# Last stage of a graph layer: every quad as fp32r halves, and the scaled x stored once in fp32

## The reference

```python
def lap_mul(A, x):
    d = 1.0 / sqrt(sum(A, axis=-1))
    return d[:, None] * (A @ (d[:, None] * x))

z = leaky_relu(lap_mul(A, x) @ W1 + b1, 0.1)
d2 = max(sq[:, None] + sq[None, :] - 2 * z @ z.T, 0)   # sq: row sums of z * z
S = exp(-sqrt(d2 + 1e-10) / 2)                       
S = where(rank of S in its row < 4, S, 0)              # the four nearest nodes
out = layernorm(x + lap_mul(S + A, x) @ W2 + b2)
```

## Time and profile before

| | us |
|---|---|
| Median of 3 runs | 2693.22 (2692.01 to 2697.63) |
| Span of the profiled execution | 2759.5 |
| of it, last stage (first rounding to the end) | 2242 to 2760 |
| TensorE busy in the span | 90% |
| VectorE busy in the span | 84% |
| ScalarE busy in the span | 58% |
| GpSimd busy in the span | 43% |

### The profile page before, as it was taken

One profiled execution on the slowest core, in us unless ns is written; L12 is line 12 of the kernel. 1 busy time (PEld: TensorE's weight loads), 2 busy tenths in 40 slices (PEclk: granted clock), 3 DMA queues, 4 the chain that ended last, 5 costly groups with the idle time before them and its releaser, 6 DMA issues.

```text
span 2759.5 us, 29107 instructions
## 1 busy us (share of the span) xinstructions
PE 2482.6 (90%) x9356; PEld 1722.4 (62%) x9356; DVE 2319.8 (84%) x1411; ACT 1606.7 (58%) x1905; POOL 1195.4 (43%) x987
## 2 busy tenths in 40 slices
PE   1367999999999998899999999999999987888978
PEld 0133444444677776578787877778787764666655
DVE  7998899977788888999999999999999773666766
ACT  0000000000477767999989899899988763555655
POOL 0000000000000000377778878788878956666760
PEclk9688999999999999999999999999999988999989
DMA  9999999995899960146555655555655688988975
GB/s 385 421 402 408 398 421 421 421 421 215 320 349 342 338 226 7 35 141 183 151 163 138 179 142 175 140 170 149 174 143 167 182 309 343 347 324 320 345 295 208
DMA packets 147949, 718.58 MB, mean 260 GB/s; under 512 B 19025, under 2 KB 26961, under 8 KB 86609
## 3 DMA queue, kind: packets, MB, share of 16 engines
q1 hardware_dynamic: 124384, 670.49, 65.6%
q0 software_dynamic: 18800, 37.77, 5.7%
q10 hardware_dynamic: 4608, 8.39, 0.8%
HBM read 680.40 MB, written 36.18 MB: 260 GB/s over the span
## 4 chain that ended last, share of the span: by engine, by line
PE 56%; issue 10%; ACT 10%; DVE 9%; DMA 7%; POOL 3%; another core or an unknown queue 3%; SPq 0%; ACTq 0%; POOLq 0%; DVEq 0%
PE PS L767 17%; PE PS L866 5%; PE PS L868 5%; PE PS L867 5%; DMA ring<-at 4%; ACT R L1141 3%; PE PS L834 3%; PE PS L910 3%; PE PS L921 3%; PE PS L911 3%; PE PS L830 2%; PE PS L831 2%; ACT ah_t L1191 2%; DVE R L1621 2%
## 5 line engine op out<-in xcount | busy, mean ns | idle before, releaser
L1299 POOL TENSOR_TENSOR al<-ring,ah 128x1024 fp32r<-128x1024 f32 x264 | 644.0, 2441 | 180.5 <-ACT ah L1112 168.7
L1621 DVE MAX8 R<-R 128x8 f32<-128x8192 f32 x64 | 555.9, 8685 | 68.1 <-ACT R L1141 67.9
L1141 ACT ACTIVATE R<-PS 128x1024 f32<-128x1024 f32 x512 | 518.1, 1018 | 114.1 <-PE PS L874 83.1
L1624 DVE FIND_INDEX8 R<-R,R 128x8 uint32<-128x8192 f32 x64 | 555.9, 8685 | 0.3 <-issue 0.3
L1272 POOL CAST zst<-zh 128x128 fp32r<-128x128 f32 (+1 forms) x64 | 26.2, 410 | 1113.2 <-DVE zl L1556 811.5
L866 PE MATMUL PS<-zh,zst 128*128 128x512 f32 x1024 | 407.3, 398 | 28.6 <-ACT PS L1127 12.7
L868 PE MATMUL PS<-zh,zst 128*128 128x512 f32 x1024 | 400.4, 391 | 0.0
L867 PE MATMUL PS<-zl,zst 128*128 128x512 f32 x1024 | 400.1, 391 | 0.0
L1456 POOL DMA_INDIRECT R<-xs_dram,R x256 | 279.7, 1093 | 145.2 <-issue 75.5
L1127 ACT ACTIVATE PS<-R 128x1024 f32<-128x1024 f32 x310 | 318.0, 1026 | 6.6
L1046 ACT ACTIVATE tiny<-rowsum 128x4 f32<-128x4 f32 x16 | 3.3, 205 | 481.2 <-DVE rowsum L1491 481.2
(11 more groups left out here) (177 smaller groups left out, 4469.9 us busy)
## 6 DMA issues: line engine op xcount, KB each, us to landing
R<-at SPq DMA_DIRECT2D x152, 1024.0 KB, 13.3
ring<-at SPq DMA_DIRECT2D x148, 1024.0 KB, 9.5
ring<-at SPq DMA_DIRECT2D x264, 512.0 KB, 3.9
cache<-at SPq DMA_DIRECT2D x117, 1024.0 KB, 20.2
raw_sq<-at SPq DMA_DIRECT2D x21, 1024.0 KB
raw_z<-at SPq DMA_DIRECT2D x20, 1024.0 KB
raw_ring<-at SPq DMA_DIRECT2D x20, 1024.0 KB
acc_dram<-R POOLq DMA_DIRECT2D x78, 256.0 KB, 5.7
```

The source lines that it names most:

```text
L1141: act.activation(score[j % 2][:, c * EC:(c + 1) * EC].rearrange("p (b c) -> p b c", b=2), pair(first, j, c), ACT.Copy).then_inc(copied, 1)
L1299: pool.tensor_tensor(al[:, k % SPLIT], raw[k % RAW], ah[:, k % SPLIT].bitcast(F32), ALU.subtract)\
L1621: v.max(top[:, j], score[j % 2]).then_inc(dve3, 1)
L1624: v.max_index(place[:, j], top[:, j], score[j % 2]).then_inc(placed, 1)
```

## The change

1. All 124 quads of the last stage are halved. The plain branch is gone, and with it the bookkeeping of places. For the last group, ACT makes the high half of xg (`high_of_last`, after quad 4's rounding) and DVE the low half (`low_of_last`, ahead of quad 5's).
2. In the third stage, SP writes the scaled x of a group twice in fp32 (once in the layout for the gathers, once as it lies on chip, `xp_dram`) in place of once plus both halves, and reads the next x only when both have landed. POOL's wait for the writes of the halves is gone.
3. In the last stage, SP reads one 512 KB piece for a group in place of two. ACT makes its high half (`high_of_xs`), POOL its low half (`low_of_xs`) in place. POOL's six later low halves stand between its other work: two ahead of the write of the last group's x, one ahead of the gathers, and three behind the 4th, 16th and 28th gather.

```diff
+LOW_AFTER = {4: (0, 0), 5: (0, 3), 6: (1, 2)}
...
-                        dst = xh_dram[bass.ds(g, 1)].rearrange("o p t d -> p (o t) d")
-                        sp.dma_start(dst, xgh_g[:, :, :].bitcast(F32)).then_inc(s_split, 16)
-                        dst = xl_dram[bass.ds(g, 1)].rearrange("o p t d -> p (o t) d")
-                        sp.dma_start(dst, xgl_g[:, :, :].bitcast(F32)).then_inc(s_split, 16)
+                        dst = xp_dram[bass.ds(g, 1)].rearrange("o p t d -> p (o t) d")
+                        sp.dma_start(dst, xg).then_inc(s_xp, 16)
                     if k == RAW + (NP0 // 2 if first else 0):
                         sp.wait_ge(s_xg, 16 * (g + 1))
+                        sp.wait_ge(s_xp, 16 * (g + 1))
...
             def load_t(u):
-                if u >= RAW_T and plain[u - RAW_T]:
-                    sp.wait_ge(prod_t, u - RAW_T + 1)
-                elif u >= RAW_T:
+                if u >= RAW_T:
                     wait_rest(sp, u - RAW_T)
...
             def load_xs(g):
-                sp.dma_start(xsh[:, g * GT:(g + 1) * GT].bitcast(F32), xh_dram[g]).then_inc(s_xs[g], 16)
-                dst = (xsl if g < G - 2 else xsh)[:, low * GT:(low + 1) * GT].bitcast(F32)
-                sp.dma_start(dst, xl_dram[g]).then_inc(s_xs[g], 16)
+                sp.dma_start(low_tiles(g).bitcast(F32), xp_dram[g]).then_inc(s_xs[g], 16)
...
             def quad(u):
-                if plain[u]:
-                    pe.wait_ge(xg_ok, chain_of(G - 1, False))
-                    pe.wait_ge(ld_t[u % RAW_T], 16 * (u // RAW_T + 1))
-                    for k in range(TB):
-                        i = pe.matmul(bank, xg[:, (h * TB + k) % GT], raw_t[u % RAW_T][:, k], ...)
-                    i.then_inc(prod_t, 1)
-                    return
-                pe.wait_ge(s_xs[h * TB // GT], 32)
-                pe.wait_ge(rnd_t, n + 1)
+                if h >= LAST:
+                    pe.wait_ge(xl_last_ok, 1)
+                else:
+                    pe.wait_ge(xs_low, h * TB // GT + 1)
+                pe.wait_ge(rnd_t, u + 1)
...
+            def high_of_last():
+                act.wait_ge(xg_ok, chain_of(G - 1, False))
+                act.activation(xgh_of[1][:, :, :], xg, ACT.Copy).then_inc(xh_last_ok, 1)
+            def high_of_xs(g):
+                act.wait_ge(s_xs[g], 16)
+                act.activation(xsh[:, g * GT:(g + 1) * GT], low_tiles(g).bitcast(F32), ACT.Copy).then_inc(xs_high, 1)
+            high_of_xs(0)
             for u in range(len(tail)):
-                if not plain[u]:
-                    round_t(u)
+                round_t(u)
+                for g in range(1, G - 1):
+                    if u == tail.index((HB, g * GT // TB)) - 1:
+                        high_of_xs(g)
...
+                if u == BY_POOL + 2:
+                    high_of_last()
...
-                    pool.wait_ge(s_split, 32 * (g - 1))
-                    hold(pool)
...
+            def low_of_xs(g):
+                pool.wait_ge(xs_high, g + 1)
+                pool.tensor_tensor(low_tiles(g), low_tiles(g).bitcast(F32), xsh[:, g * GT:(g + 1) * GT].bitcast(F32),
+                                   ALU.subtract).then_inc(xs_low, 1)
+            low_of_xs(0)
             for u in range(BY_POOL):
...
+            low_of_xs(1)
+            low_of_xs(2)
             pool.wait_ge(xg_ok, chain_of(G - 1, False))
             pool.dma_start(dst.rearrange("(t p) d -> p t d", p=P), xg).then_inc(s_xg_last, 16)
+            low_of_xs(3)
...
+                    for g, after in LOW_AFTER.items():
+                        if (f, j) == after:
+                            low_of_xs(g)
...
+            def low_of_last():
+                v.wait_ge(xh_last_ok, 1)
+                v.tensor_tensor(xgl_of[1][:, :, :], xg, xgh_of[1][:, :, :].bitcast(F32), ALU.subtract)\
+                 .then_inc(xl_last_ok, 1)
...
+                if u == BY_POOL + 3:
+                    low_of_last()
-                if not plain[u]:
-                    rest_t(u)
+                rest_t(u)
```

More of the change, by code:

```diff
@@ L126, in plan_tail, with build @@
     return quads
-def build(nc, x, at, W1, b1, W2, b2, consts, out, xs_dram, xh_dram, xl_dram, acc_dram):
+def build(nc, x, at, W1, b1, W2, b2, consts, out, xs_dram, xp_dram, acc_dram):
     loads, products, two = plan_ab()
@@ L288, in build, with high_tile, low_tiles @@
             raw_t.append(sb(name, [P, TB, BC], at=where)[:, :, :])
+        def high_tile(t):
+            return xsh[:, t] if t < (G - 1) * GT else xgh_of[1][:, t % GT]
+        def low_tiles(g):
+            low = g if g < G - 2 else G - 1
+            return (xsl if g < G - 2 else xsh)[:, low * GT:(low + 1) * GT]
         def low_tile(t):
+            if t >= (G - 1) * GT:
+                return xgl_of[1][:, t % GT]
             return xsl[:, t] if t < (G - 2) * GT else xsh[:, t + GT]
@@ L376, in build @@
         flushed = sem("flushed")
-        s_split = sem("s_split")
+        s_xp = sem("s_xp")
+        xs_high = sem("xs_high")
+        xs_low = sem("xs_low")
         s_xs = [sem(f"s_xs{k}") for k in range(G - 1)]
@@ L391, in build @@
         acc_seeded = sem("acc_seeded")
+        xh_last_ok = sem("xh_last_ok")
+        xl_last_ok = sem("xl_last_ok")
         rnd_t = sem("rnd_t")
@@ L521, in build @@
         n_heavy = [f + 1 - n_light[f] for f in range(B)]
-        plain = [h >= LAST for b, h in tail]
-        halved = [u for u in range(len(tail)) if not plain[u]]
-        place_of = {u: n for n, u in enumerate(halved)}
         def wait_rest(eng, u, part_=RESTS - 1):
-            if place_of[u] < BY_POOL:
-                eng.wait_ge(al_pool, place_of[u] + 1)
+            if u < BY_POOL:
+                eng.wait_ge(al_pool, u + 1)
             else:
-                eng.wait_ge(al_dve, RESTS * (place_of[u] - BY_POOL) + part_ + 1)
+                eng.wait_ge(al_dve, RESTS * (u - BY_POOL) + part_ + 1)
         def wait_halves_free(eng, u):
-            if place_of[u] >= 2:
-                eng.wait_ge(prod_t, halved[place_of[u] - 2] + 1)
+            if u >= 2:
+                eng.wait_ge(prod_t, u - 1)
         def wait_yf(eng, f):
@@ L986, in quad @@
                         wait_rest(pe, u, k * RESTS // TB)
-                    i = pe.matmul(bank, xsh[:, h * TB + k], al_t[n % 2][:, k], start=False, stop=False,
-                                  skip_group_check=True)
+                    i = pe.matmul(bank, high_tile(h * TB + k), al_t[u % 2][:, k], start=False,
+                                  stop=last and k == TB - 1, skip_group_check=True)
                 i.then_inc(prod_t, 1)
@@ L1190, in round_t @@
                 wait_halves_free(act, u)
-                act.activation(ah_t[place_of[u] % 2][:, :, :], raw_t[u % RAW_T], ACT.Copy).then_inc(rnd_t, 1)
+                act.activation(ah_t[u % 2][:, :, :], raw_t[u % RAW_T], ACT.Copy).then_inc(rnd_t, 1)
+            def high_of_last():
+                act.wait_ge(xg_ok, chain_of(G - 1, False))
+                act.activation(xgh_of[1][:, :, :], xg, ACT.Copy).then_inc(xh_last_ok, 1)
             def load_xb(f):
@@ L1662, in rest_t @@
             def rest_t(u):
-                n = place_of[u]
-                v.wait_ge(rnd_t, n + 1)
+                v.wait_ge(rnd_t, u + 1)
                 wait_halves_free(v, u)
@@ L1767 @@
     xs_dram = nc.dram_tensor("xs_dram", (N, D), F32, kind="Internal").ap()
-    xh_dram, xl_dram = (nc.dram_tensor(n, (G, P, GT, D), F32, kind="Internal").ap() for n in ("xh_dram", "xl_dram"))
+    xp_dram = nc.dram_tensor("xp_dram", (G, P, GT, D), F32, kind="Internal").ap()
     acc_dram = nc.dram_tensor("acc_dram", (len(ROWS_0), P, BC), F32, kind="Internal").ap()
-    build(nc, **ins, out=out, xs_dram=xs_dram, xh_dram=xh_dram, xl_dram=xl_dram, acc_dram=acc_dram)
+    build(nc, **ins, out=out, xs_dram=xs_dram, xp_dram=xp_dram, acc_dram=acc_dram)
     r = run_bass_kernel_spmd(nc, [arrays], core_ids=[0])
```

14 lines of the change are left out of this document (4 added, 10 removed).

## The result

| | us | ratio to before, 95% |
|---|---|---|
| before, median | 2693.22 (2692.01 to 2697.63) | |
| after, median | 2727.48 (2725.93 to 2728.92) | 1.0124 (1.0112 to 1.0136) |

The account below looks back on a forecast made before the run. When data flows, PE, DVE and DMA were taken to be full at once, PE first. The terms, -3 at the start and +14 later, gave +11 on the median of 2693: 2704 us, range 2674 to 2726.

Parts of the forecast that it names:

- the dense piece: Last stage, 2610 to 2656, without holes: PE busy 97%, DVE 90%, DMA share 0.96.
- the cover: Start of the last stage: DVE's idle time beside late loads hides the first 8 quads' added work; without it, another 20 us.
- The plain quads, first eight: Last stage, part that waits for loads: halving these 8 quads adds ACT and DVE work costed at nothing.
- The other 24: Later plain quads of the last stage: half fall in dense pieces at 1.2 us each, +14 us; bounds 0 and 29.
- The start: Last stage before quad 19: up to 9 us earned by fewer reads, only 3 kept; bounds 9 kept, 8 lost.
- The gate: POOL's low half for quad 19, behind 28 gathers and three low halves, ready at 2328.5, some 3 us below today's rounding.
- DVE held up by POOL's low halves: Last stage: each of six later low halves could block DVE for one POOL instruction, 16 us, left out of the sum.
- The third stage: SP's wait for the second write before reading the next x: covered by 140 us, costed at nothing.
- (1): Rival: DMA covers everything later, the added 14 us are nothing and 9 us are earned: 2684 us, chance 0.20.
- (2): Rival: PE was the true bound and DVE keeps up: -17 to -26 us, about 2671 us, chance 0.10.
- (3): Rival: with two buffers each rounding waits for the product two quads back: +29 us later, 2722 us, chance 0.17.
- What was to show it: Signs in the changed trace: 124 roundings, DVE 79 us busier, PE waiting for POOL at quads 15 and 19.

Follow-up runs that it names:

- e12: Kernel before with only the first 8 plain quads halved, both halves of x stored and read as before: 2694.99 us, ratio 1.0000.
- the second profile: The kernel before, unchanged, profiled once more: span 2696.1 us, against 2759.5 in the first profile.
- e2: Kernel before with all 124 quads halved, both halves of x stored and read as before: 2718.21 us, ratio 1.0085.
- e3: Kernel before with 16 of its 32 plain quads halved, both halves of x stored and read as before: 2706.00 us, ratio 1.0044.
- e13: e7 with ACT's root of the variance, the normalising and the block's x load each two quads later: 2708.23 us, ratio 1.0049.
- e4: Changed kernel with the low halves of x for groups 4, 5 and 6 made by DVE instead of POOL: 2716.23 us, ratio 1.0083.
- e1: Kernel before with x stored and read once in fp32, halves made on chip, the 32 plain quads kept: 2696.27 us, ratio 1.0007.
- e7: e2 with low halves written over the raw quads, giving four high-half buffers; raw buffers refilled after the product: 2718.08 us, ratio 1.0089.
- e8: e2 with less DVE layernorm work: no bias b2, mean and variance from one of four tiles: 2700.71 us, ratio 1.0027.

## Why the prediction was wrong in size

**What bounds the kernel now.** The reading of the dense piece was right, that of the stretch around it was not. The text took 0.91 of DMA share, 89% of PE and 72% of DVE for the kernel's usual state, and the 63 us of late loads for part of it. It noted that the span was 66.3 us above the median, and made the sum "as a difference between two kernels", as if the difference were free of them. It was not: the cover that it counted on was the late loads' own.

**The plain quads, first eight: nothing.** Right. e12 gives +1 (-2 to +3). Their cover is the kernel's own: the second profile has all of its waits for loads before 2400.

**The other 24: half in dense pieces, 12 x 1.2 = 14.** This is one of the two steps that failed: 24 us measured for 14, which is 10 of the 23 that the forecast is short. It has two factors. The share was wrong: every one of the 24 counts (e2, e3), since the stretch is dense from end to end. The price was about right, 1.0 measured (24 us for 24 quads), inside its bounds of -0.70 and +2.44. Its reason was not: "DVE can be as full as PE was (97%)". By that rule on the second profile DVE would need 213.7 + 16.6 x 2.36 = 253 us of 260, just 97%, and the 24 would cost next to nothing. DVE got 90%. What it lacks are the waits in the ring with ACT and PE, of which the place of the layernorm in ACT's order is up to 9 us (e13). So two errors offset each other in the 1.2: a stretch taken for emptier, and a DVE taken for fuller than it can be.

**The start: -3.** This is the other step that failed, and the larger: +9 measured (changed kernel against e2), 12 us of the 23, and beyond the bound of 8 lost. The gate was named rightly and its time put wrongly, in three ways. It was compared with quad 19 at 2331.9, which is 2322.5 without late loads. The low half for quad 19 was put at 2328.5 and ended at 2335.4: the first gather went at 2283.7 and not at 2280, since the low half for group 3 took 4.08 us and stood behind ACT's; and the 28 gathers took (2332.9 - 2283.7 - 2.49 - 2.35) / 28 = 1.58 each with the waiting, not 1.31. And the gate at quad 15 was not computed at all. By the forecast's own terms it is 2280 + 16 x 1.31 + 4 + 2 x 2.62 = 2310.2, against a rounding that ends at 2307.6: late even so. It ended at 2316.3. Besides, the 9 us of saved reads are not kept even without the gates: in e4 ACT's waits for gathered rows, which the forecast named only in its bound, take most of them.

**DVE held up by POOL's low halves.** The forecast quoted a rule and put up to 16 us of DVE's time on it. The trace shows 10.6. DVE's timeline of the changed kernel, with POOL's low halves at 2267.23 to 2269.76, 2313.93 to 2316.28 and 2332.90 to 2335.39:

```profile
2266.30 4.55 DVE L1688 TENSOR_TENSOR al_t<-raw_sq,ah_t 128x1024 fp32r<-128x1024 f32 x2 [0.83 <-PE PS L985]
...
2313.48 3.08 DVE L1704 TENSOR_TENSOR R<-R 128x256 f32<-128x256 f32 x1
...
2323.86 2.36 DVE L1688 TENSOR_TENSOR al_t<-raw_ring,ah_t 128x1024 fp32r<-128x1024 f32 x2 [6.97 <-ACT ah_t L1189]
2326.14 0.42 DVE L1704 TENSOR_TENSOR R<-R 128x256 f32<-128x256 f32 x1
...
2333.12 2.56 DVE L1704 TENSOR_TENSOR R<-R 128x256 f32<-128x256 f32 x1
```

The line that takes 0.42 us alone takes 3.08 and 2.56, and both times it ends 0.3 us after POOL does. A pair of low halves takes 4.55 in place of 2.36. By the rule of the Trainium skill (page "SBUF — State Buffer", section "Who interferes with whom"), that such a pair of engines shares a port and one is blocked for the other's whole instruction, the trace agrees; the forecast also took from it that the second to start is the one blocked, and this the trace doesn't bear out, since DVE's addition at 2313.48 has the earlier start by 0.45 us. Over five of the six it comes to some 2.2 + 1.4 + 2.2 + 2.7 + 2.1 = 10.6 us; the sixth met a search. DVE's busy time over the span agrees: 2403.6 us against 2393.1 in e2. It was not counted in the sum "in a part where it idles". Whether it moved the end is not settled: e4 takes three of the six away together with the gathers ahead of them. Little speaks for it: behind the hold at 2313.48 DVE idles 6.97 us for a rounding, and the holds ahead of it lie ahead of a gate whose time POOL sets.

**The third stage: nothing.** Right as far as seen. e1, which has all of it, is within 0.2%, and its first rounding is at 2247.7, behind the high half of group 0 (1.06 us), against 2246.0 in the second profile.

**The rivals.** (1), that DMA covers everything, is out: 1.00 of share before fell to 0.97 with fewer bytes a second. (2), that PE is the bound and DVE keeps up, is half true: PE was the fullest engine at 96%, and no engine waited for a load in the long stretch; but DVE doesn't keep up. (3), "the chain of two buffers", named +29 for the later quads, the nearest figure to the 24. Its buffers were not the cause (e7); the clause "DVE, whose layernorm work stands in between" was part of it (e8, e13).

**What was to show it.** PE waits for POOL at quads 15 and 19: seen, 8.5 and 5.1 us, and with 21 us in all above the 10 that were to tell the forecast wrong. Roundings 124, yes. DVE's busy time is 2403.6 against 2319.6 over the span, +84 for +79, of which 10 are time that POOL held it. DVE at 95% in a dense piece with PE below it: only in two of the thirteen stretches of 20 us from 2400 to 2660 (98.7% and 95.2%). The best of them:

```profile
2500.00:2520.00 20.00, 18.74 (x85) 14.04 (x85) 19.73 (x36) 14.82 (x20) 15.73 (x15) 1.00 0.97 350
```

DMA's share below 0.91 in the long stretch: no, 0.97, from 1.00. The mark was set from the disturbed profile; in GB/s the fall is 8%.

## What to carry to other kernels

Hold the span of the profile against the median of the runs before reading any share from it. Where they differ by more than the runs scatter, the idle time in the trace may be that one execution's, and an edit that seems to be covered by it is not. Here a piece without holes was then the better picture of the whole.

Three engines that hand each other one item after the next, each with work of its own in a fixed order between, may not reach the fill of one alone: here the fullest, DVE, had 90%, where PE had 96 before. So time moved off a full engine must be counted at the fill that the ring will have, and the place of each side task in each order is a term of its own.

Work put into an in-order queue behind slow issues (here, 28 gathers) is a due time for each item. Compute it for every item, not for the last one only, and with the durations that hold when the neighbours are busy. Time earned ahead of such a queue is kept only up to the next item that is due from it: in e4 9 us of lead fell to 2.7 in waits for gathered rows.

## What the runs showed that was not expected

- Two profiled executions of one unchanged kernel were 63 us apart. In the longer one ACT has nine waits called `remote` (one of 17.7 us), five of them in the long stretch; the other has none of these, and no wait for DMA there.
- The time of a POOL subtraction of 128 by 1024 beside DVE's: 4.08 us for the one that met two pairs, 2.35 to 2.56 for others. DVE's 128 by 256 addition, 0.42 alone, took up to 3.08. By the records DVE's addition at 2313.48 began before POOL's subtraction and was held all the same, so it can't be said from them which engine wins.
- Most of DVE's time counts at 90% busy: 20.5 us of its work removed gave 17.5 us (e8).
